# One broadcast DMA in place of repeated row loads, and the store ahead of the load, in the window attention of a four-stage attention and mixture-of-experts kernel

## The reference

```python
q = apply_rope((layernorm(x) @ q_w.T + q_b) ...) * d ** (-0.5)   # 16 sequences, 16 heads, 512 x 16
k = apply_rope((ctx @ k_w.T + k_b) ...)
v = (ctx @ v_w.T + v_b) ...
idx = q_pos + arange(-64, 1)                  # each query sees its own position and the 64 before it
scores = einsum('bhqd,bhqwd->bhqw', q, k[idx])
e = exp(scores - max(scores)); probs = e / sum(e)
out = einsum('bhqw,bhqwd->bhqd', probs, v[idx])
```

## Time and profile before

| | |
|---|---|
| median of 3 runs | 6166.09 us (6157.45 to 6167.23) |
| the profiled execution | 6167.23 us, of which the span is 6165.5 us |
| PE, PEld, DVE, ACT, POOL busy over the span | 83%, 44%, 52%, 41%, 17% |
| mean granted TensorE clock | 0.91 |
| `window_attention` | about 468 to 969 us of the span |

### The profile page before, as it was taken

One profiled execution on the slowest core, in us unless ns is written; L12 is line 12 of the kernel. 1 busy time (PEld: TensorE's weight loads), 2 busy tenths in 40 slices (PEclk: granted clock), 3 DMA queues, 4 the chain that ended last, 5 costly groups with the idle time before them and its releaser, 6 DMA issues. The chain is left out here.

```text
span 6165.5 us, 88753 instructions
## 1 busy us (share of the span) xinstructions
PE 5124.5 (83%) x27631; PEld 2717.2 (44%) x27632; DVE 3176.9 (52%) x6296; ACT 2503.8 (41%) x3173; POOL 1018.8 (17%) x786
## 2 busy tenths in 40 slices
PE   6778996699458999999999999999964089999970
PEld 3435664444224444443444444444343056666650
DVE  4556763211337888887888788888734000000013
ACT  1223552112114777776776677777620011111110
POOL 3440002311330000000000000000023700000016
PEclk8888998899778999999999999999876589999985
DMA  6445665700565333333333333333154421111115
GB/s 216 121 119 156 164 164 164 217 24 24 141 174 78 61 62 61 67 67 66 67 67 67 55 51 62 62 67 57 28 159 149 139 69 65 52 52 49 56 58 183
DMA packets 363364, 579.30 MB, mean 94 GB/s; under 512 B 56576, under 2 KB 258751, under 8 KB 360816
## 3 DMA queue, kind: packets, MB, share of 16 engines
q1 hardware_dynamic: 344976, 523.46, 35.7%
q0 software_dynamic: 14768, 50.51, 2.3%
q10 hardware_dynamic: 3264, 0.79, 0.1%
HBM read 297.72 MB, written 197.24 MB: 80 GB/s over the span
## 5 line engine op out<-in xcount | busy, mean ns | idle before, releaser
L1180 DVE TENSOR_REDUCE full_peak<-full_item 128x1 f32<-128x512 f32 (+2 forms) x3392 | 2036.2, 655 | 481.0 <-PE full_item L1247 475.4
L1150 ACT ACTIVATE full_prob<-full_score 128x1024 f32<-128x1024 f32 (+1 forms) x1792 | 1649.9, 960 | 659.9 <-PE full_score L1258 653.6
L1247 PE MATMUL full_item<-full_kst,full_qst 49*128 49x512 f32 (+1 forms) x4096 | 1205.2, 407 | 55.3 <-DVE full_peak L1180 23.8
L1258 PE MATMUL full_score<-full_qst,full_kst 51*128 51x512 f32 (+1 forms) x3328 | 1112.8, 448 | 17.3 <-ACT full_prob L1150 11.9
L1258 PEld LDWEIGHTS full_score<-full_qst,full_kst 51*128 51x128 f32 (+1 forms) x3328 | 481.1, 183 | 932.2 <-ACT full_prob L1150 600.6
L1272 PE MATMUL full_value<-full_prob,full_vaug 128*17 128x512 f32 x6656 | 887.0, 605 | 0.8 <-ACT full_raw L1137 0.7
L1247 PEld LDWEIGHTS full_item<-full_kst,full_qst 49*128 49x128 f32 x4096 | 630.5, 189 | 200.3 <-DVE full_peak L1180 129.4
L2069 ACT ACTIVATE moe_hT<-moe_hbank,moe_b 128x512 f32<-128x512 f32 (+1 forms) x320 | 199.4, 623 | 806.6 <-PE moe_hbank L2124 802.1
L2136 PE MATMUL moe_ybank<-moe_w,moe_hT 128*128 128x256 f32 x2176 | 485.1, 384 | 5.2 <-ACT moe_hT L2069 5.2
L2124 PE MATMUL moe_hbank<-moe_xT,moe_w 128*128 128x512 f32 (+1 forms) x1280 | 477.5, 531 | 6.4 <-DMA moe_b<-in_b 6.4
L2136 PEld LDWEIGHTS moe_ybank<-moe_w,moe_hT 128*128 128x128 f32 x2176 | 414.7, 192 | 67.3 <-issue 6.0
(11 more groups left out here) (207 smaller groups left out, 5282.2 us busy)
## 6 DMA issues: line engine op xcount, KB each, us to landing
full_kst<-full_high SPq DMA_DIRECT2D x256, 200.1 KB
full_ctxT<-in_ctxT SPq DMA_DIRECT2D x16, 1601.0 KB, 9.1
full_kst<-full_low SPq DMA_DIRECT2D x128, 200.1 KB
win_qst<-scratch_q SPq DMA_DIRECT2D x384, 64.0 KB, 2.6
full_qst<-scratch_q SPq DMA_DIRECT2D x384, 64.0 KB
scratch_xbuf<-ctxp_zero POOLq DMA_DIRECT2D x17, 1024.0 KB
scratch_attn<-win_raw SPq DMA_DIRECT2D x64, 256.0 KB, 2.1
scratch_q<-open_parts SPq DMA_DIRECT2D x128, 128.0 KB, 2.3
```

Source lines behind the costliest of these rows:

```text
L1150: nc.scalar.activation(prob[h][(s.par * PAIRS + t) % 2][0:rows, 0:banks, :], score[u % 2][0:rows, 0:banks, :], ACT.Exp, scale=SCALE).then_ ...
L1180: nc.vector.tensor_reduce(peak[s.par][:, hq:hq + len(qts), c], src, AX, ALU.max).then_inc(item_read, 1)
L1247: ins = nc.tensor.matmul(ps[:, at:at + z - a], qst[s.slot][rows, h // 2, qt * P:(qt + 1) * P].bitcast(F32R), kst[s.slot][rows, h // 2, a:z ...
L1258: ins = nc.tensor.matmul(score[u % 2][0:z - a, kt % 2, :], kst[s.slot][rows, h // 2, a:z].bitcast(F32R), qst[s.slot][rows, h // 2, :].bitc ...
```

## The change

`load` issues one DMA where it issued three (query part 0) and one where it issued two (query part 1): the source is given a leading dimension with step 0 that repeats the part. The third one, of part 2, has a leading dimension of 1. The number of DMAs that a stack is counted to have falls from nine to six. In `window`, the store of window s-1 with its wait now stands ahead of the loads and no longer behind them.

```diff
-        STACK_DMAS = 3 + 6
+        STACK_DMAS = 3 + 3
...
                 for part, times in ((0, 3), (1, 2), (2, 1)):
-                    for _ in range(times):
-                        sp.dma_start(q[at:at + HD, :, :].rearrange("r h k -> r (h k)"),
-                                     srq[part * HD:(part + 1) * HD]).then_inc(into, 16)
-                        at += HD
+                    rows = times * HD
+                    sp.dma_start(q[at:at + rows, :, :].rearrange("r h k -> r (h k)"),
+                                 srq[part * HD:(part + 1) * HD].unsqueeze(0).broadcast_to([times, HD, GROUP * SQ])).then_inc(into, 16)
+                    at += rows
...
                 if not first:
                     sp.wait_ge(score_full, UNITS * s.n)
                     sp.sem_inc(carry, 1)
+                    store(s.plus(-1))
                 if s.group == 0 and left >= GROUP:
                     sp.wait_ge(vaug_done, s.n + 1)
                     load_values(s.batch + 1, (s.k // GROUP + 1) % 2)
                 if left >= LOADS_AHEAD:
                     load(s.plus(LOADS_AHEAD))
-                if not first:
-                    store(s.plus(-1))
```

## The result

The changed kernel takes 6352.42 us, median of 3 runs (6346.86 to 6362.45), against 6166.09 before: a ratio of 1.0309, 95% interval 1.0284 to 1.0334. It is slower by 186 us. I had forecast slower, 6220 us, with a range up to 6290. The direction and the cause, few DMA engines, held; the size didn't, and one effect, PE's clock, was missing from the sum. The profiled execution is a fourth one, 24 us above the median: 6376.07 us, with a span of 6374.3.

A forecast was written before the change was run, and what follows sets the result against it. PE's own order was taken to bound the stage, 7.31 us a window. Late loads, 5.0 us at the start plus 58 windows of 0.92, gave +58 us, 6224, rounded down to 6220 us; range 6185 to 6290.

The forecast's parts named there:

- What bounds the kernel, and the move of the store: Touched stage: PE's order sets 7.31 us per window; the moved store leaves a load 8.45 us instead of 15.8.
- Few engines for the new DMAs: Merged query loads: sources of outermost 3 and 2 run on three and two DMA engines, 4800 fewer small packets.
- I take 25.2: Rate per DMA engine in GB/s for the new query loads: engines 0 and 1 need 7.5 us per window.
- the slow rate: Rival: DMA engines in the stage run at 16.8 GB/s each, 11.2 us a window, 6290 to 6400 us; chance 0.07.
- L = 9.83: Microseconds from a copy's end to its following load's landing, against 8.45 available: late by 1.4; 10.74 with a value load.
- The clock should stay: PE in the touched stage: stays at full clock despite waits, as at 960 us with PE busy for 65%.
- I-to-V: Time from a window's first `max` item on PE to the end of ACT's value copy: taken as 6.17 us.
- the signs that I listed: Expected in the trace: PE waits for query loads nearly every window, about 0.9 us on average; copies 8.2 us apart.
- The parity argument: Value loads always fall on windows of one parity, which sets the pace: four windows last 32.91 us, one 8.23.
- my sum (201 against 58): Whole touched stage: 5.0 us at the start plus 58 windows of 0.92 us, 53.4, together +58 us.
- The start: First loads of the stage: stack 0 late by 2.4 us, rising to +5.0 at stack 5.
- a rate of 20 GB/s: Slow bound, a fifth below 25.2 per engine: 9.4 us a window, +122 us, the range's upper end.

The follow-up runs named there:

- e1: The kernel before with only the store moved ahead of the loads, query loads still six DMAs of 16 rows: 6169.93 us, ratio 1.0011.
- e3: The changed kernel with stack rows ordered row by row, so the outermost dimension is 16 and the step-0 dimension second: 6165.84 us, ratio 1.0005.
- e5: The changed kernel with the repeated query source replaced by distinct blocks of 16 rows that follow one another: 6166.41 us, ratio 1.0001.
- e9: The changed kernel with query DMAs reading every third (second) row, distinct blocks that can't join into one run: 6354.87 us, ratio 1.0316.
- e2: The kernel before with only the broadcast query DMAs, the store still behind the loads: 6250.5 us, ratio 1.0143.
- e7: The changed kernel with LOADS_AHEAD 7 instead of 5: 6245.39 us, ratio 1.0133.
- e11: The changed kernel with loads seven ahead and without the third key and query DMAs (16 rows each) from window 8 on: 6209.33 us, ratio 1.0079.
- e10: The changed kernel with the three key DMAs only for the first eight windows, later windows using stale keys: 6249.18 us, ratio 1.0133.
- e6: The changed kernel, five ahead, without the third key and query DMAs (16 rows each) from window 8 on: 6323.8 us, ratio 1.0255.
- e8: The changed kernel with 20 extra matmuls on PE ahead of the wait for a stack in every second window: 6311.05 us, ratio 1.0228.

## Why the prediction was wrong

**What bounds the kernel, and the move of the store: right.** PE's order set the pace. The store ahead of the loads takes 7.31 us of lookahead and costs little by itself (e1, 8 us; I had put it at nothing).

**Few engines for the new DMAs: right**, to the packet (4800), by e3 and e5 against e9. The rule of the Trainium skill ("DMA: Bandwidth & Descriptors", "Rules for kernel authors") holds here for 2 and 3, and e5 adds that blocks which join don't count as a dimension.

**"I take 25.2": mis-sized.** The rate of one undisturbed engine was right (78 GB/s on three). But I used it for a whole load and a whole window, in which transfers of all 16 engines run beside. What was 7.5 us of work per window measured 8.24 (e2, e7). Of the excess of 0.7, the loads of 16 rows are 0.2 (e7 and e11). I had seen the slow rate in the earlier trace rows and given it a chance of 0.07 as all or nothing; the truth lay between.

**L = 9.83: mis-sized, and the larger part of the loss.** It measured 12.14, and 14.41 with values where I had 10.74. The terms, roughly and partly overlapping: the lead-in of a broadcast DMA (2.1 us in place of 0.88 in e10; in the full kernel some 1.3, as the keys run meanwhile), 0.9 us that go with the keys (e10), and what the 16-row loads add (e6, 29 us in all or 1.0 in two windows, their bytes and the clock included). The load with values, 3.7 us above my sum, wasn't taken apart.

**"The clock should stay": the step that failed.** I read from the earlier trace rows that PE was busy for 65% at 960 us and still at full clock, and took I-to-V as 6.17 whatever happened, even at most shrinking. But a share over 10 us says nothing of one long gap. My own sum spread the stalls evenly, 0.9 us a window, and the signs that I listed had PE wait in nearly every window. The parity argument beside it said that one window in two takes all of it, 1.85 us, and with L larger it became 3.4 to 6.1. Behind all 27 waits of 3.4 us and more the clock fell, and I-to-V became 7.6 to 9.0. e8 gives 41 us back by keeping PE at work. The 6.17 itself was right: behind the shorter waits it measured 6.16, and not the 5.9 that I allowed for. This also couples the terms: a late load lengthens the wait, the wait slows the clock, the slow windows put off the next copy and with it the next load. So an L that was too small cost twice.

**The loss by its terms.** The stage of the profiled run is 142 us longer than my sum (201 against 58). The clock, a term that I had put at nothing, is 57 of them, the start 7, and the remaining 78 are put down to the longer L. The same account of e8, where PE is kept at work, has 106 us above the sum: 19, 8 and 79. The clock's share falls, that of L stays.

By medians, the order alone costs 8 us, the broadcast alone 88, both 186. The 90 that belong to neither part alone come where loads with 8.45 us to land meet slow engines. How they divide between late loads and clock isn't separated, as e2 has nine I-to-V times lengthened by the clock too, by 15 us in all.

**The start: right in kind, short in size.** I had +5.0 us by the sixth stack. The first copy came 12.4 us late. Already the first stack is there at 491.3 and not at 486.7, beside a value load that took 11.8 us to land, and from 487 us on SP's issue of three query DMAs takes 4.8 to 5.8 us in place of 2.2, so SP is held up itself.

**Range.** Its upper end was a rate of 20 GB/s, 122 us. With most of the clock's cost removed the time is 6311 (e8), 21 past that end; the 19 us of clock that e8 keeps are nearly all of these 21. So the end allowed for about what the longer L costs, by a rate of 20 GB/s where 22.9 was measured (184 KB in 8.24 us), and for nothing of the clock. I had also written that copies 9 us or more apart would mean a misjudged rate. They came 10.17 apart, and the rate alone makes 8.24 (e2, e7): that sign didn't tell a low rate from a long L and a lost clock. Left open is where the transfers slow each other, in DRAM or where they write: no run here tells it. Also open is why the lead-in of a broadcast DMA is longer.

## What to carry to other kernels

Before two DMAs are merged, write down the outermost dimension of both sides: 3 and 2 copies of 16 rows as [3, 16, n] and [2, 16, n] ran on three and two engines and cost 1.4% of the kernel by themselves and 3% together with a shorter lookahead. As [16, 3, n] and [16, 2, n] they cost nothing. Count the small packets in the trace to see which it is. Lookahead hides a late load only while the busiest DMA engine gets through its bytes in a period; here it didn't, and two more windows of lookahead just moved the wait to the store. And when a sum predicts waits, ask how long a single one is and not how large their share: a wait of PE of 3.6 us was followed by some 6 us at about half the clock, which cost 2.5 us more.

## What the runs showed of the hardware that was not expected

- PE's granted clock fell to 0.50 at the end of a wait of 3.6 us (still 1.00 from 712 to 714, 0.72 from 714 to 716, 0.50 from 716) and was back at 1.00 only at 722, 6 us after work had started at 716.1.
- A DMA on three engines moved its first data about 2.1 us after issue (e10), a store on 16 engines after 0.88. Its issue also takes longer on SP, 0.67 us at the median of all query issues and the same in e9. But e3's, on 16 engines and with a dimension that doesn't join either, take 0.57, and e5's, which join, 0.37, as the plain ones of before do. So the issue time doesn't go with the number of engines alone.
- The queue has memory: with seven ahead a store of 256 KB, which landed after 2.1 us at the median before, lands after 14.3 and became the thing that ACT waits for (65.3 us in 39 waits). That its share on the first engines stands behind the query rows there is my reading; no view shows a single engine.
- An access of [3, 16, n] whose blocks follow one another runs on 16 engines (e5: 341904 packets on q1), the same shape with a step of one row between its blocks on three (e9: 340176).
- The length of a wait alone did not tell whether the clock was lost behind it: in e6, waits of 1.7 and 1.8 us were followed by an I-to-V time of 7.7 us (the granted clock was 0.59 and 0.56 in the 4 us from 557, behind the first of them), and others of 2.5 to 3.1 by 6.2.
